# Attention kernel: the transposed probabilities of a step in one two-bank PSUM tile, evacuated by one ScalarE and one VectorE operation in place of two each

## What is computed

```python
energy = jnp.einsum('nhqd,nhkd->nhqk', q, k)
attn = jax.nn.softmax(energy / np.sqrt(HEAD_DIM), axis=3)
out = jnp.einsum('nhql,nhld->nhqd', attn, v)
```

## Time and profile before

| | |
|---|---|
| runs | 2871.25, 2878.01, 2882.04 us, median 2878.01 |
| span of the profiled execution | 2876.8 us, 1.2 us under the median of the runs |
| busy share PE / DVE / ACT / POOL | 90% / 69% / 60% / 31% |
| mean granted TensorE clock | 0.961 of full |
| attention stage of one image, first to last turn | 204.9 us, eight times |

### The profile page before, as it was taken

How to read it: one execution, slowest core, us unless ns; L and a number is a source line. 1 busy time by engine, 2 the same in 40 slices (tenths; PEclk the granted TensorE clock), 3 DMA queues, 4 the chain that set the end, 5 groups by cost and what they waited for, 6 DMA issues and landing times. The chain is left out here.

```text
span 2876.8 us, 37893 instructions
## 1 busy us (share of the span) xinstructions
PE 2576.8 (90%) x13344; PEld 2089.4 (73%) x13344; DVE 1994.2 (69%) x3636; ACT 1736.2 (60%) x3048; POOL 901.6 (31%) x804
## 2 busy tenths in 40 slices
PE   4899898998899988999889989899898998999976
PEld 3788667876578766887668867688666886678864
DVE  4688656886478863887638876488765887568853
ACT  3677436773377734777347763477635775367742
POOL 0244303443034330443304433144321444124420
PEclk9999999999999998999989999999999999999997
DMA  6223102231113211222112221222302323032300
GB/s 232 59 75 117 74 19 82 78 103 74 55 46 88 92 73 60 59 70 92 74 60 67 73 97 58 61 69 73 142 10 71 77 63 143 1 88 70 92 30 30
DMA packets 79976, 215.55 MB, mean 75 GB/s; under 512 B 9968, under 2 KB 10256, under 8 KB 74000
## 3 DMA queue, kind: packets, MB, share of 16 engines
q1 hardware_dynamic: 79760, 212.77, 24.3%
HBM read 103.68 MB, written 25.17 MB: 45 GB/s over the span
## 5 line engine op out<-in xcount | busy, mean ns | idle before, releaser
L1035 POOL TENSOR_SCALAR PR_loop<-PR_loop,rinv_loop 128x1024 f32<-128x1024 f32 x448 | 504.0, 1125 | 1264.5 <-DVE rinv_loop L1000 1264.3
L1028 DVE TENSOR_TENSOR PL_loop<-pT_loop,PH_loop 128x512 fp32r<-128x512 f32 x896 | 577.0, 686 | 212.9 <-ACT PH_loop L980 209.8
L980 ACT ACTIVATE PH_loop<-pT_loop 128x512 fp32r<-128x512 f32 x896 | 487.3, 596 | 314.4 <-PE pT_loop L905 310.2
L995 DVE TENSOR_REDUCE nmax_loop<-pS_loop 128x1 f32<-128x1024 f32 x448 | 545.5, 1218 | 124.6 <-PE pS_loop L895 119.5
L950 ACT ACTIVATE PR_loop<-pS_loop,nmax_loop 128x1024 f32<-128x1024 f32 x448 | 501.1, 1119 | 23.5 <-DVE nmax_loop L995 21.2
L905 PE MATMUL pT_loop<-ident,PR_loop 128*128 128x128 f32 x3584 | 467.6, 273 | 18.0 <-POOL PR_loop L1035 17.8
L905 PEld LDWEIGHTS pT_loop<-ident,PR_loop 128*128 128x128 f32 x3584 | 415.0, 141 | 93.3 <-POOL PR_loop L1035 40.9
L894 PE MATMUL pS_loop<-KHL,QS 128*128 128x512 f32 x896 | 368.5, 411 | 57.8 <-issue 52.6
L926 PE MATMUL pO_loop<-PH_loop,VS 128*128 128x512 f32 x896 | 361.4, 403 | 40.7 <-DVE OT L1019 40.7
L927 PE MATMUL pO_loop<-PL_loop,VS 128*128 128x512 f32 x896 | 358.9, 401 | 0.0
L895 PE MATMUL pS_loop<-KHL,QS 128*128 128x512 f32 x896 | 357.7, 399 | 0.0
(11 more groups left out here) (284 smaller groups left out, 4078.1 us busy)
## 6 DMA issues: line engine op xcount, KB each, us to landing
KHL<-HL_loop SPq DMA_DIRECT2D x168, 256.0 KB, 3.6
WQ<-wqk_split SPq DMA_DIRECT2D x64, 512.0 KB, 5.8
QS<-HL_loop SPq DMA_DIRECT2D x168, 128.0 KB, 3.1
X<-in_x SPq DMA_DIRECT2D x32, 512.0 KB, 9.4
WO<-wo_split SPq DMA_DIRECT2D x16, 1024.0 KB, 6.6
X_loop<-in_x SPq DMA_DIRECT2D x28, 512.0 KB, 5.0
KHL<-wv_split SPq DMA_DIRECT2D x14, 1024.0 KB, 10.0
out<-X_loop SPq DMA_DIRECT2D x14, 1024.0 KB, 7.8
```

The source lines that it names most:

```text
L980: act.activation(PH[ck % 2][:, 4 * half:4 * half + 4, (g % 4) * P:(g % 4 + 1) * P], pT[half][:, :].rearrange("p (k n) -> p k n", k=4), ACT ...
L995: dve.tensor_reduce(nmax[:, g:g + 1], pS[g % 2][:, :], AX.X, ALU.max, negate=True)\
L1028: dve.tensor_tensor(PL[ck % 2][:, ks, qs], pT[half][:, :].rearrange("p (k n) -> p k n", k=4), f32(PH[ck % 2][:, ks, qs]), ALU.subtract).th ...
L1035: pool.tensor_scalar(PR[g % 2][:, :], PR[g % 2][:, :], rinv[:, g:g + 1], 1.0, ALU.mult, ALU.mult)\
```

## The change

The two PSUM tiles of 512 columns become one tile of 1024 columns that covers the same two banks. PE transposes all eight blocks and signals once. One ACT operation copies the 1024 columns and one DVE operation subtracts the 1024 columns, each with one semaphore increment. The counts in all waits on a_tr, a_hi and a_lo are halved with it.

```diff
-        pT = [c.enter_context(nc.psum_tensor(f"pT{i}_{tag}", [P, 512], F32)) for i in range(2)]
+        pT = c.enter_context(nc.psum_tensor(f"pT_{tag}", [P, HW], F32))
...
                 pe.wait_ge(S["a_norm"], g + 1)
-                for half in range(2):
-                    if g >= 1:
-                        pe.wait_ge(S["a_lo"], 2 * (g - 1) + half + 1)
-                    for k in range(4):
-                        kb = 4 * half + k
-                        mm = pe.transpose(pT[half][:, k * P:(k + 1) * P], PR[g % 2][:, kb * P:(kb + 1) * P],
-                                          ident[:, :])
-                    mm.then_inc(S["a_tr"], 1)
+                if g >= 1:
+                    pe.wait_ge(S["a_lo"], g)
+                for kb in range(ST):
+                    mm = pe.transpose(pT[:, kb * P:(kb + 1) * P], PR[g % 2][:, kb * P:(kb + 1) * P], ident[:, :])
+                mm.then_inc(S["a_tr"], 1)
...
-                    pe.wait_ge(S["a_lo"], 8 * (ck + 1))
+                    pe.wait_ge(S["a_lo"], 4 * (ck + 1))
...
-                    act.wait_ge(S["a_tr"], 2 * (g - 1))
+                    act.wait_ge(S["a_tr"], g - 1)
...
-                    for half in range(2):
-                        act.wait_ge(S["a_tr"], 2 * g + half + 1)
-                        act.activation(PH[ck % 2][:, 4 * half:4 * half + 4, (g % 4) * P:(g % 4 + 1) * P],
-                                       pT[half][:, :].rearrange("p (k n) -> p k n", k=4), ACT.Copy)\
-                           .then_inc(S["a_hi"], 1)
+                    act.wait_ge(S["a_tr"], g + 1)
+                    act.activation(PH[ck % 2][:, :, (g % 4) * P:(g % 4 + 1) * P],
+                                   pT[:, :].rearrange("p (k n) -> p k n", k=ST), ACT.Copy).then_inc(S["a_hi"], 1)
...
-                    for half in range(2):
-                        ks = slice(4 * half, 4 * half + 4)
-                        qs = slice((g % 4) * P, (g % 4 + 1) * P)
-                        dve.wait_ge(S["a_hi"], 2 * g + half + 1)
-                        dve.tensor_tensor(PL[ck % 2][:, ks, qs], pT[half][:, :].rearrange("p (k n) -> p k n", k=4),
-                                          f32(PH[ck % 2][:, ks, qs]), ALU.subtract).then_inc(S["a_lo"], 1)
+                    qs = slice((g % 4) * P, (g % 4 + 1) * P)
+                    dve.wait_ge(S["a_hi"], g + 1)
+                    dve.tensor_tensor(PL[ck % 2][:, :, qs], pT[:, :].rearrange("p (k n) -> p k n", k=ST),
+                                      f32(PH[ck % 2][:, :, qs]), ALU.subtract).then_inc(S["a_lo"], 1)
```

## The result

The changed kernel takes 3124.28 us (median of 4 runs, 3115.96 to 3127.66) against 2877.55 us: a ratio of 1.086, 95% interval 1.0839 to 1.0882. It is 8.6%, 247 us, slower. The forecast was 3111 us with a range of 3080 to 3185. The profiled execution is the fastest of the four, 3115.96 us with a span of 3114.2; the sum of the prediction gave a span of 3110.6.

The account below looks back on a forecast made before the run. PE was taken to bound the middle of a stage, while the lengthened way round of 3.51 us sets 39 steps an image. Adding 29.2 us an image, 233.8 in all, to the 2876.8 us span gave 3111 us, range 3080 to 3185.

Parts of the forecast that it names:

- PE bounds the middle, the evacuations are idle: Mid attention stage: PE busy all 122.36 us, the evacuations idle before they run, so cheaper ones gain nothing.
- The way round c: From one turn's start to the next through PE, ACT, DVE and back: no step shorter than 3.51 us.
- The two unknown operations: ACT's copy and DVE's subtraction of 1024 columns, put at 1.03 and 1.22 us.
- the restart of PE: From the end of DVE's subtraction to PE's next turn, taken as 0.09 us from waits of 0.06 and 0.12.
- Rival 3: DVE's 1024-column subtraction takes 1.51 us in place of 1.22, giving 3212 us; chance 6%.
- The sum by steps: Added time over the steps of one image's attention stage and its end: 29.2 us an image, 234 us for eight.
- held at 4.24: First step of groups without projections, set by the wait for OT, expected to keep some 4.24 us.
- The end of a stage: After an image's last turn, OT begins 3.34 us later in place of 2.56: +0.78 us.
- From the span to the runs: Whole program: the median of the runs stands 1.2 us above the span, 3110.6 us.
- Not slower: Rival: PE's work covers the way round in every step; 36 us saved at most, 2842 us; chance 5%.
- slower by less: Rival: some of the three parts overlap or a step has unseen slack, 2892 to 3080 us; chance 3%.
- The clock: Rival: waits in the sparse steps cost PE its full clock, 2.4 GHz for 1.2, giving 3219 us; chance 8%.

Follow-up runs that it names:

- e5: The changed kernel with the two waits ahead of PE's turn in the other order, subtraction first, then scaling: 3102.95 us, ratio 1.0779.
- e1: Kernel before with one 1024-column tile, every operation still in halves, the next turn waiting for both halves: 2915.48 us, ratio 1.0129.
- e2: Kernel before with only PE's signal merged, one after all eight transposes; copies, subtractions and freeing stay in halves: 2928.92 us, ratio 1.0184.
- e3: Kernel before with only DVE's subtraction merged to 1024 columns, the next turn waiting for all of it: 3014.81 us, ratio 1.0474.
- e4: Kernel before with one PE signal and one ACT copy of 1024 columns; DVE subtracts and frees in halves: 3011.98 us, ratio 1.0474.
- e8: Changed kernel without the projections of heads 2 to 7, values matmuls and their evacuation, with two 1024-column tiles used in turn: 2682 us, one run.
- e12: The stripped kernel with two wide tiles (e8), with DVE's reciprocal moved ahead of the row maximum: 2500 us, one run.

## Why the prediction was right

- **PE bounds the middle, the evacuations are idle.** Right: ACT and DVE lost 30 and 42 us of work and nothing was gained.
- **The way round c.** It was put at 3.51 us as 1.13 + 1.03 + 0.04 + 1.22 + 0.09. In the stretch from 547.95 it is 1.16 + 1.03 + 0.03 + 1.225 + 0.147 = 3.59, and at the start of an image 3.53. The two unknown operations were right to 5 ns: 1027 and 1225 ns. The mis-sized term is the restart of PE, 0.09 for 0.147. The 0.09 was read up to PE's weight load, and up to there it is 0.116; the turn is counted from its first multiplication, 0.03 later. The first part has to do with the order of the two waits: with the other order it is 0.053 (e5).
- **The price of the longer subtraction.** Rival 3 took 1514 ns from the subtraction with both operands in SBUF. That is a mean, and the kernel before has this spread of it (ns, shortest, median, longest):

```profile
L375 DVE TENSOR_TENSOR OL_loop<-OT,OH_loop x28: 1216/1302/2356, 316.0 to 2444.3; 128x1024 fp32r<-128x1024 f32 x28
```

The shortest is as long as the 1225 ns of the change, so the mean was no price for the work on 1024 columns. POOL was at work during the longest ones, but during some of the shortest too; what lengthens them was not tested.

- **The sum by steps.** Predicted against measured, in us an image: steps 0 to 7 +5.58 and +5.80; 8 to 11 +1.69 and +1.51; the nine steady groups +12.15 and +13.4 (13.62 to 15.11); 48 to 51 +1.95 and +2.07; 52 to 59 +4.50 and +4.2; 60 to 62 +2.58 and +2.3. Together +28.5 and +29.3. The first step of the groups without projections (the steps from turns 8, 52, 56 and 60) was held at 4.24; it went down to 3.86, since DVE now has the subtraction behind it when the turn starts and so is through with OT 2.25 us after the turn in place of 2.62. That is 12 us in eight images. It is opposite to the error of the restart and hides part of it, which is luck.
- **The end of a stage.** OT begins 3.36 us after the last turn in place of 2.56, +0.80 for +0.78. But the stretches between the images grew by 0.6 us on average, and the start and the end of the program took 1.5 us less, so outside the stages 2.4 us were added in all where the sum had 6.2. The stages added 235.0 us where it had 227.6. These two errors cancel to 3.6 us.
- **From the span to the runs.** The profiled execution is within 4 us of the sum. The other three runs are 8 to 12 us longer than the profiled one; no profile of them was taken, and where that lies is open. Their granted clock was 0.960 to 0.961, that of the profiled one 0.962.
- **The rivals.** Not slower, or slower by less, are ruled out by the time and by the 312 turns that wait for the subtraction; the longer subtraction by its 1225 ns. The clock: the granted clock is 0.962 for the whole and 1.00 in the sparse steps, as these rows of the changed kernel show (columns as in the earlier trace rows), so the clock did not fall. The Trainium skill says that transposes do not count as PE-busy in the same way ("TensorE: Matmul & The Clock Gate", the part on PE-mode transpose); nothing in these rows shows it:

```profile
514.10:640.00 125.90, 116.51 (x637) 94.87 (x638) 91.00 (x117) 85.42 (x124) 47.75 (x42) 1.00 0.25 64
478.40:506.70 28.30, 22.34 (x125) 17.24 (x124) 19.64 (x25) 18.33 (x27) 10.27 (x9) 1.00 0.12 28
```

- **What each part costs.** e1 and e2 cost 37 and 50 us, e3 and e4 136 and 133, all of it 247. The parts don't add up, since a step is as long as the longest of its ways round: c was worked out for each as 2.76, 2.76, 3.19 and 3.19, and the times expected from it were within 8 us of those measured. Part of that closeness is luck: within the stages 35, 46, 119 and 125 us were added where the sums had 45, 45, 129 and 129. In e1 and e3 the first step of the sparse groups fell to 3.88 us as in the change (12 us), and in e3 the stretches outside the stages made up for it. What is bought with a merged operation is 0.07 us of DVE's time (its pair takes 1.29, the one operation 1.225); what is paid is the overlap of that operation with the one before and the one behind it.

## What to carry to other kernels

When a buffer is passed from engine to engine and back, add up the way round: start of the producer to its next start, each operation and each hand-over. A merge of two operations into one lengthens it even where every engine gets less work, and it costs in those steps alone whose own work is shorter than the way round; so compare it with the shortest steps, not with the mean. If it can't be shortened, give each step the same amount of the bounding engine's other work (here that won 60 us with the long way round and 33 us with the short one). Where two waits stand ahead of one instruction, write the one that is satisfied last first: here that won 21 us.

## What was not expected of the hardware

- The order of two semaphore waits ahead of one PE instruction is worth 0.06 us each time. From the end of DVE's operation to PE's first weight load it is 0.116 us with the later wait written second, 0.053 us with the later wait written first; the step falls from 3.59 to 3.53 us.
- A merged operation can hurt a second way through the list of its engine with no buffer in it: 5.87 us for two steps in e8, gone when two independent instructions changed places (e12).
